# A two-layer decoder: GpSimd multiplies by the reciprocal sums in cross-attention's softmax, VectorE takes only the reciprocals, and the instruction orders are written anew

## The reference, cut to what matters

```python
q, k = _rmsnorm(q, qn_w), _rmsnorm(k, kn_w)
scores = einsum('bhsd,bhtd->bhst', q, k) * scale + mask
attn = softmax(scores, axis=-1)        # exp(s - max) / sum
out = einsum('bhst,bhtd->bhsd', attn, v)
...
y = out @ Wo
```

## Time and profile before

| | |
|---|---|
| median of 3 runs | 892.48 us |
| the profiled execution's time | 891.87 us |
| its span | 890.1 us |
| TensorE matmul (PE) | 820.7 us busy, 92% |
| TensorE weight load (PEld) | 638.7 us, 72% |
| VectorE (DVE) | 699.6 us, 79% |
| ScalarE (ACT) | 506.9 us, 57% |
| GpSimd (POOL) | 298.2 us, 33% |

### The profile page before, as it was taken

One profiled execution on the slowest core, in us unless ns is written; L12 is line 12 of the kernel. 1 busy time (PEld: TensorE's weight loads), 2 busy tenths in 40 slices (PEclk: granted clock), 3 DMA queues, 4 the chain that ended last, 5 costly groups with the idle time before them and its releaser, 6 DMA issues.

```text
span 890.1 us, 14401 instructions
## 1 busy us (share of the span) xinstructions
PE 820.7 (92%) x5004; PEld 638.7 (72%) x5004; DVE 699.6 (79%) x1719; ACT 506.9 (57%) x1283; POOL 298.2 (33%) x314
## 2 busy tenths in 40 slices
PE   6866989799999999999999999999999999999984
PEld 5744766687787777877777776877678867778763
DVE  2677788988997998788889679887898978576554
ACT  4356125357527864378625884258752677668763
POOL 1413735322643145413354024611444134112100
PEclk9878999999999999999999999999999999999999
DMA  8672010010010000100001000010000000000000
GB/s 286 220 263 91 25 25 24 1 25 13 1 24 1 24 2 13 25 13 13 13 1 25 13 13 13 1 36 1 13 1 1 13 1 1 2 13 0 14 1 24
DMA packets 37063, 28.65 MB, mean 32 GB/s; under 512 B 18688, under 2 KB 34560, under 8 KB 36608
## 3 DMA queue, kind: packets, MB, share of 16 engines
q1 hardware_dynamic: 36992, 27.74, 10.0%
HBM read 25.64 MB, written 2.10 MB: 31 GB/s over the span
## 4 chain that ended last, share of the span: by engine, by line
PE 59%; DVE 23%; issue 7%; ACT 7%; DMA 2%; POOL 1%; DVEq 0%; SPq 0%; POOLq 0%; ACTq 0%
PE bank L1312 8%; PE bank L1273 8%; PE bank L1301 5%; PE bank L1005 5%; PE bank L1291 5%; PE bank L1192 4%; PE bank L1074 3%; PE bank L1076 3%; PE bank L1077 3%; DVE S L933 2%; PE bank L1296 2%; PE bank L1106 2%; PE bank L1171 2%; DVE amax L827 2%; PE bank L1279 1%
## 5 line engine op out<-in xcount | busy, mean ns | idle before, releaser
L638 ACT ACTIVATE S<-S,mx 128x128 f32<-128x128 f32 x256 | 99.4, 392 | 59.0 <-DVE mx L936 58.5
L1273 PE MATMUL bank<-XTE,w_xq 128*128 128x256 f32 x512 | 122.2, 381 | 0.4 <-ACT QA L630 0.4
L1312 PE MATMUL bank<-w_xo,OX 128*128 128x256 f32 x512 | 116.0, 380 | 0.0
L1273 PEld LDWEIGHTS bank<-XTE,w_xq 128*128 128x128 f32 x512 | 94.7, 190 | 16.8 <-ACT QA L630 2.0
L362 POOL TENSOR_TENSOR rq<-vq,minus_half 128x8 f32<-128x8 f32 x32 | 53.6, 1675 | 157.8 <-DVE vq L924 157.6
L1312 PEld LDWEIGHTS bank<-w_xo,OX 128*128 128x128 f32 x512 | 95.9, 190 | 14.6 <-issue 2.3
L629 ACT ACTIVATE QS<-bank,per_partition_sb 128x256 f32<-128x256 f32 x128 | 60.4, 472 | 61.5 <-PE bank L1273 61.0
L933 DVE SCALAR_TENSOR_TENSOR S<-bank,rq,xmask 128x128 f32<-128x128 f32 x256 | 71.8, 342 | 26.9 <-PE bank L1291 24.6
L260 POOL TENSOR_TENSOR prod<-XTA,ccolA 128x256 f32<-128x256 f32 x96 | 59.4, 650 | 38.9 <-DVE prod L260 20.4
L1291 PEld LDWEIGHTS bank<-KTX,QA 128*128 128x128 f32 x512 | 63.2, 192 | 11.1 <-issue 9.8
L1291 PE MATMUL bank<-KTX,QA 128*128 128x128 f32 x512 | 68.0, 278 | 0.6 <-ACT OX L647 0.5
(11 more groups left out here) (222 smaller groups left out, 1807.2 us busy)
## 6 DMA issues: line engine op xcount, KB each, us to landing
xin<-in_x SPq DMA_DIRECT2D x8, 256.0 KB, 2.7
taps_sb<-in_taps SPq DMA_DIRECT2D x1, 2048.0 KB, 11.5
cnat<-in_ctx SPq DMA_DIRECT2D x8, 256.0 KB, 2.7
ccolA<-in_ctxT SPq DMA_DIRECT2D x32, 64.0 KB, 2.7
ccolE<-in_ctxT SPq DMA_DIRECT2D x16, 128.0 KB, 2.3
w_xq<-in_L_xattn_Wq SPq DMA_DIRECT2D x1, 2048.0 KB, 12.4
w_xo<-in_L_xattn_Wo SPq DMA_DIRECT2D x1, 2048.0 KB, 17.2
out_x<-X SPq DMA_DIRECT2D x8, 256.0 KB, 2.1
```

Of the source, the lines that this page charges most:

```text
L638: ins = nc.scalar.activation(S[:, b, seq(h)], S[:, b, seq(h)], ACT.Exp, bias=mx[:, b, h:h + 1], accum_out=sm[:, b, h:h + 1])
L1273: ins = nc.tensor.matmul(cols(EQ)[:, h], w_xq[:, k, hh * XDIM:(hh + 1) * XDIM], XTE[:, k], start=k == 0, stop=k == HALVES - 1)
L1312: ins = nc.tensor.matmul(rows(EY)[:, b], OX[:, h, b], w_xo[:, n * XGROUP + h], start=n == 0 and h == 0 and b == 0, stop=n == XKV - 1 and h ...
```

## The change

The reciprocal at L939 now signals `e_rs0` or `e_rs1`. The multiplication, with the same operands and in place, becomes a step of its own on GpSimd, which waits for that signal and sends `e_p0` or `e_p1` to TensorE as before. GpSimd's order therefore gains 32 letters x and 32 letters y. The orders of all five queues are written anew; each but GpSimd's has the same number of each letter as before.

```diff
@@ gpsimd
+            def scores(g, b):
+                s3 = S[:, b].rearrange("p (h t) -> p h t", h=XGROUP)
+                for n in range(XKV):
+                    yield
+                    gp.wait_ge(sems[f"e_rs{b}"], nth(g, XKV, n))
+                    sig(gp.tensor_tensor(s3, s3, rs[:, b].unsqueeze(2).broadcast_to([P, XGROUP, P]), ALU.mult), f"e_p{b}")
+
-            together(ORDER["pool"], s=set_up(), a=station_a(front, ffn), c=each_group(middle), q=station_q(keys, queries), o=each_group(output))
+            together(ORDER["pool"], s=set_up(), a=station_a(front, ffn), c=each_group(middle), q=station_q(keys, queries),
+                     x=each_group(lambda g: scores(g, 0)), y=each_group(lambda g: scores(g, 1)), o=each_group(output))
@@ vector, scores(g, b)
-                    order(nc.vector.reciprocal(rs[:, b], sm[:, b]))
-                    sig(nc.vector.tensor_tensor(s3, s3, rs[:, b].unsqueeze(2).broadcast_to([P, XGROUP, P]), ALU.mult), f"e_p{b}")
+                    sig(nc.vector.reciprocal(rs[:, b], sm[:, b]), f"e_rs{b}")
@@ ORDER (the last lines of TensorE's, GpSimd's whole, SP's whole)
-        "yaxcqcyqoqccqyxaqcyqcyqxaacqxyoyqayqxaqxaxayqayxqoqyxaqxoyqaayaxqxyqxoqyaxyqxyaxqoqyxayxayxoayxaxaya"
+        "xcaqcxqycoqyxqcyqxcqxcoqycqxyaaqyxqaxqoqyxaqyxyqoqyxaqyayqaxqaxyqaxyqoaaqyaxqaxxoayaxyaxyaxoayxayaax"
         "aoaaaaaaaaa"
-        "sasaaaaaaacsaccaqaacaqacaacaqcqcaaacaacaqcqcaaccqcqcaaqcaaaaqcqaqcoqcccaqcacqaacaqaaaqqcaoqcccqacacq"
-        "caacacqaacaqqoaqcqaacqcqacqaqocaaaaqcaccqqacaqcqqcaaoqcaaaacaccqcqcqoqcqqccacqqoqaqqaoa"
+        "sasaaaaaaacsaqcqcaaacaqacqaccacaqcyxcaaqacayqcxaacaycaqcyxqcaaxcaoaqcaacyxqcaqycxcqxycaqacqyxcqaaxca"
+        "qaqaayoqacxyccqyxacaqxcyqcaaqacoqayaaxqcacyxcqyxcqayaxcqcaaqocqayaxaaqcaccyxqxyaqcayxcqaaqcaqaoyaaqc"
+        "xcxcaycqxycqycxqycxoqqycqxcyxcqyxaqyoqxyqxqayxyxaoa"
-        "asssaqsassassaqaqaaaaqoaaqoaaqoaaqoqoooo"
+        "asssaqsassassqaqaaaaaqoaaqoaaqoaaqoqoooo"
```

More of the change, by code:

```diff
@@ L157, in build_decoder @@
             d_xT d_xTc d_kvr d_r d_k d_kv d_rs d_kd d_st d_o d_mp d_q d_vp d_ve d_rstd d_n d_nTc d_y
-            e_kv e_kc e_vc e_ks e_vk e_kn e_kT e_kTc e_xT e_xTc e_q e_qc e_ssq e_vq e_rq
+            e_kv e_kc e_vc e_ks e_vk e_kn e_kT e_kTc e_xT e_xTc e_q e_qc e_rs0 e_rs1 e_ssq e_vq e_rq
             e_sc0 e_sc1 e_mx0 e_mx1 e_e0 e_e1 e_p0 e_p1 e_pT0 e_pT1 e_pTc0 e_pTc1 e_o0 e_o1 e_oc0 e_oc1 e_y e_u
@@ L1329 @@
     "pe": (
[L1330 to L1336, removed]
+        "sassasaaasaaaaaaaasaaascqccaqccaaqaqaqcqqaacccaaqacaccacaacqcaqcaqqqqcqcayqxcacaqcyqayxqaycxxoccaacq"
+        "aqacaqccacayacyaacyqaxqcxyqxyoqyaqcacayqycaxqaxcxocaqaxyqxcqaoccacaaqaxcaccacaqcyxaycqxyxocaqayqxayx"
+        "aqyxqcaqcoaaqcaqacxqyxcqxyqyqoaqaqaccqcycxqayxqacxqcaaqcaaayaqacaqaaqcxyoqcaxqyxqyoqcqayxqayxaqycxac"
+        "qaoqaayqaacqxyxcyxocaqaqcaxqyxyccqacaqxyoacqacaaacaqaacaqacxqyxqcayqyxcaqoaqyxaqyacxacqyxqoaqcaayxqa"
+        "yxcqyxocqyqaxyqaaccqcacaqxyxcocaaqccaaqaaaqaacacqyxqyaqcqaxyaxoqayxqyaxqaxqcyoqaacxqaacqyxycxyoqcayq"
+        "aqayqacxayccxcqxaqaoaaqaaqcaacqccxyqaxcyxcqayqcaqoxqyxaqyxcyqcoqcyxaqcyxqayxcqoyqycaxqyxccxqcoyqyxqy"
+        "xcaqcxqycoqyxqcyqxcqxcoqycqxyaaqyxqaxqoqyxaqyxyqoqyxaqyayqaxqaxyqaxyqoaaqyaxqaxxoayaxyaxyaxoayxayaax"
         "aoaaaaaaaaa"
@@ L1339 @@
     "dve": (
[L1340 to L1344, removed]
@@ L1345 @@
-        "qayqcacaycaxoqxaacoacaaaaaaaacaaaacaaacxcaxyacycccxqyxycacxcxyqcaycacccqyxoqyxacqcaqcaoxqxycyccccyca"
-        "aycaxcxqyayaxaxaqaayxyoxqaaoayxyxqyaxyxqaayxyaxaaaaaooaaaaaaaaa"
+        "aasssassaaasaassaaaaaaaaaaasaasaasasassaccasaqccqqcaccacacacaqaccaacaqaaaaqaccacaacaacacaacacaccaacq"
+        "cyxacyxacccaccaqcacaycaxayaqaaxaccaacaaacaaaacaycayacacqcacyxyaxcacqacxaxcccaccaaocaqacaaoacaqayaaxa"
+        "yacxacacaacqacqcayxycxcacaqcayaxaacxacyacaqaccaccycxqayxccacqaxaqxaaqccaaaqaayaaaacaayaaaacaqoaoxacy"
@@ L1347 @@
+        "xcycccacaqyaxayaacaxacaqacxayxcccyccqacaqcacyaqxaqaoyxacaoaaaacaaaaaacaqaacacacayxcyxccacaaaqyxacyax"
+        "acaqcyxayaxcacccqcaqaccacyxayqoxqocaaccaaaaaaaaaqaaacaacaacaaccyaxycxcaaqaxyaaxcayacqaaxycayxcccqacc"
+        "aaqyacqcaayqxaoaaxaacaaoaaqaaacccaacxccayaxcaycaccqxyxcycacqayxcyccxccqyacxyqcxcoqoqyayxcqaaxccycyxc"
+        "cxccqyxayxaqayyooxqaxyayaqaxaaxyaqayxaxaayaxyxaaaaaaooaaaaaaaaa"
     ),
     "act": (
-        "sassaasaasasssssccsaccscccascaaaccaqqcccqqaqacaaqaqqcqcqacqcccccqcxqcyccqxyqxyaxaaycqxyqacaxycqcxqyc"
@@ L1350 @@
[L1350 to L1354, removed]
+        "sassaasaasasssssccsccascccaasaqcaqqcqaccccqqqqqcqcqcacacaycxqacyqcayxcxcaqyqcxccyyqyxqxycyqaqcyaxcya"
@@ L1355 @@
+        "aqcaxcxcxcyaqcxqcxccycxcyxyxqyxaqacyxayxaqqcaaqcxaqacyqccxqxycyqcqaqyaaxccqayxqayxcxcacyqqxyqxqyqxyq"
+        "qaxcyqayxacayqaacqaaxqycxycxcxcayqcaaqcxyxycaayacxcqcqxqyxqyqyaxqcaqyaxqyacxaaqcyaxqayxcqcyxcyxcqycq"
+        "ayxaaccaaxcyxcaqcqqyxqyqqaxcayxqayxqyaxaaqxcqacayqcxyxcycxyqcayqcaayaacxcxyaqxqccqcxyqxyqxqyqcxqyxay"
+        "cqxcyqcxaycqcyxacyqcxyqcyxaxcyxyyxqcyxqcaayxcqyxqqxyqxqyqyxaaxqyqxqyxyxqyqyayxaqxayqaxyaaqxyaqaxyxxa"
+        "yaxyaxayxaayxayaxaaaaaaa"
     ),
     "pool": (
-        "sasaaaaaaacsaccaqaacaqacaacaqcqcaaacaacaqcqcaaccqcqcaaqcaaaaqcqaqcoqcccaqcacqaacaqaaaqqcaoqcccqacacq"
```

## The result

The changed kernel takes 894.79 us (median of 12 runs), the kernel before, run beside it, 890.83 (median of 12). The ratio is 1.004, 95% interval 1.0026 to 1.0055: slower by 0.4%, about 4 us. The prediction said 895, slower, with 0.46 for that sign.

The account below looks back on a forecast made before the run. TensorE was taken to bound the kernel, with VectorE second. From 891.9 us, -5 + 3 + 1 + 0.5 + 0 + 3 + 0.4 made 894.8, with 0.6 for the median 895.4, called 895 us; own range 893 to 898, wider range 884 to 904.

Parts of the forecast that it names:

- close pairs: Second query products following the first too closely at eight places on TensorE: 6.6 us short, half taken, +3 us.
- VectorE near 651 us: Sign named in advance: VectorE's busy time falls from 699.6 to about 651 us.
- The product on GpSimd: Each of 64 in-place 128x512 products takes 1.02 us on GpSimd, 65 us in all (61 to 81).
- VectorE's relief: 48.2 us leave VectorE, so TensorE's waits on other VectorE work shrink by a third: -5 us, ends 0 and -14.
- The longer softmax: Softmax 0.6 us longer with the product on GpSimd, before TensorE's transposes: +3 us, ends 0 and +10.
- 12 tight places: 12 of 64 places with under 0.6 us between L940's end and TensorE's transposes; 4.2 us lost if nothing is reordered.
- GpSimd's queue: Powers and other GpSimd steps delayed behind the new products, 6 us of delays: +1 us at TensorE, ends 0 and +6.
- blocked-queue rival: Multiplications behind part c steps on GpSimd wait for L418's ScalarE input: 902 to 905 us, chance 0.12.
- Collisions: VectorE stalls when meeting GpSimd instructions: 2 us more on balance, a quarter reaching TensorE, +0.5 us, ends -1 and +3.
- lock rival: New GpSimd products hold VectorE through the shared port: VectorE loses 11 us, 898 us in all, chance 0.09.
- The new orders: All five queue orders rewritten: earlier first scores 0 (ends -4, +3), query products too close together +3 (ends 0, +6).
- The end: Last transposes and copies of the span, covered by a gelu on ScalarE: +0.4 us in case the new order lost that.

Follow-up runs that it names:

- E4: The kernel before with a 128x4 product on VectorE in place of the 128x512 one, scores left unnormalised: 886.31 us, ratio 0.9946.
- E2: The changed kernel's code (product on GpSimd) with the old orders, the 64 letters put in where the reciprocals had ended: 901.3 us, 1.0108 to the kernel before.
- E9: The kernel before with GpSimd's long products cut: L418 in four, L437 and L442 in two each: 887.08 us, ratio 0.9945.
- E11: The changed kernel with L418 cut in four and L437 and L442 in two, softmax product whole: 887.09 us, 0.9947 to the kernel before.
- E3: The changed kernel with a 128x4 product on GpSimd in place of the 128x512 one, scores unnormalised: 890.19 us, 0.9988 to the kernel before.
- E5: The changed kernel, TensorE's order only: second pair of query products moved past one to three letters at eight places: 905.97 us, 1.0167 to the kernel before.
- E8: The kernel before with 64 extra 128x512 products on GpSimd into a spare tile that nothing reads: 914.94 us, ratio 1.0268.
- E12: The kernel before with L418 alone cut in four pieces of 128x256: 887.61 us, ratio 0.9968.

## Why the prediction was right

The sign and the size came out: 895 forecast and 894.79 measured, or, against the kernel before as it ran beside each, +3 forecast and +4 measured. That the sum came so near is in good part luck: the relief (too large), the softmax (too large) and the collisions (too small) were off, and these cancelled. Of the signs named in advance the product's length, GpSimd's busy time and the waits of the close pairs came; VectorE near 651 us, a wait of 6 us or more at the transposes and waits on VectorE below 10 us did not.

- **The product on GpSimd** (1.02 us forecast) takes 1.041. Right.
- **VectorE's relief**, -5 us. The step failed twice. Busy fell to 669 us and not to 651; 10.3 us of stalls beside L457 and 3.8 more beside L418 are 14 of these 18 us. And the rule that waiting goes as busy/(1-busy) did not hold: TensorE's waits on other VectorE work did not fall (14.2 for 14.3), nor in E4 with 32.5 us less on VectorE. A relief without a price gave 5.4 us, 2.9 of it at the transposes (E4), so 2.5 for this term. Mis-sized by 2.5 to 5 us.
- **The longer softmax**, +3. The wait at the transposes is 3.2 for 3.5 us: the new orders gave it its room, the lower end. With the old orders, where nothing made room, that wait grew by 4.4 us (E2), near the 4.2 counted from the 12 tight places.
- **GpSimd's queue**, +1. The long waits of the blocked-queue rival are absent: 126 us of idle time stand before the 64 products, and behind 178 us TensorE waits for GpSimd at no other line. What the delayed powers cost through VectorE was not measured.
- **Collisions**, +0.5, with 33 us of VectorE's stalls forecast. They were 42.8 us by the sum over overlaps, 10 more than before. This is the term that was most too small; the lock rival had VectorE's 11 us right but put it at 0.09, and its 898 us were not reached. E9 and E11 show that GpSimd's long instructions carry the 4 us between the kernels: with short ones they are gone. The sum of stalls does not carry them. It is 25 us in E9 and 37 in E11 at the same time, and 35 in E2 at 901 us. Which stalls reach TensorE is not shown; that the 4 us stood beside L418, whose stalls were 18.3 and 22.1 us, is argued.
- **The new orders**, +3. The size is near E3 less E4, 3.9 us. The reason given, that close pairs leave TensorE without work, is not borne out: the waits came as forecast (3.5 us at L1280), but moving the pairs apart cost 11 us (E5), and E11 keeps the waits and is as fast as E9. That its size fits is luck. One thing that the new orders do have is more stalls beside L418, 24.0 us in E3 and 15.5 in E4; over all GpSimd lines together it is only 35 against 32. The ramp-up gained (-0.8 us up to 178 us) and the stretch behind lost (+4.8 up to 360 us); that this comes of the earlier first scores, to which the prediction gave ends of -4 and +3, was not tested.
- **The end**, +0.4: from the gelu to the end of the span it took 1.6 us less than before, so the term had the wrong sign.
- Three slips in the working: three of the nine wait rows are shown and not four; 554.7 less 44 is 511 and not 508; and 4.3 to 3.0 is 30% less, which makes -4 and not -5. None changes the forecast by more than 1 us.

The Trainium skill's rule on the exclusive port pair ("SBUF — State Buffer", the section on the two physical sides) agrees with the traces: a VectorE instruction that meets a GpSimd one waits to its end, 2.31 us for one of 0.17 above. That a shorter GpSimd instruction makes a collision cheaper is what E9 and E11 bear out, if not in proportion: L418 in four parts took the stalls beside it from 18.3 to 11.9 us in E9, in more places.

## What to carry to other kernels

An engine's busy share is no measure of what its relief is worth: VectorE with 32.5 us less to do, at no price and in the orders of before, was worth 5.4 us; TensorE was 97% busy from 178 to 860 us, and more than half of the gain was one short wait. Before moving elementwise work to GpSimd, look for small VectorE instructions with a maximum far over their median, and first cut GpSimd's long instructions; here that gave 0.5% in the kernel before, as much as the relief without its price, and it made up for the move in the changed one. In a fixed order removing a short wait can cost more than the wait (E5), so test a wait by moving one letter and read the lag of the same steps between the traces.

## What the runs showed of the hardware

- The stall is not bound to large VectorE operands or two inputs: L707, one input of 128x2 and 0.17 us, took 2.31 us beside L418.
- Four GpSimd products of 128x256 with VectorE working between them took 727 ns each at the median, where the convolution's products of that shape, with broadcast operands, take 627, and cost GpSimd 49.5 us in all for 38.6 (E9); with this cut alone the kernel was 3 to 4 us faster (E12).
- GpSimd work that nobody reads or waits for cost 24 us (E8); how much of it by VectorE's stalls (24.4 us beside it) and how much by what stood behind it in GpSimd's order is not separated.
